# Both groups of a turn finished as (x - m)(1 + k s) + m, in a kernel of group normalization, gates and a 3x3 convolution

## The reference, cut to what matters

```python
x_n = (x - mean_group(x)) / sqrt(var_group(x) + eps)
gap, gmp = mean(gx, (h, w)), max(gx, (h, w))
channel_weight = sigmoid(gn(conv1x1(concat([gap, gmp])), over channels' pixels))
pos_h, pos_w   = gates from the row means and the column means of gx
sx = conv3x3(gx * pos_h * pos_w) + b_s3
spatial_weight = sigmoid(gn(sx) )          # mean and variance per channel, w and b
out = x + gx * (channel_weight * spatial_weight)
```

## Time and profile before

| | us |
|---|---|
| three timed runs | 3390.4, 3395.1, 3396.04 (median 3395.1) |
| the profiled execution | 3391.47 |
| its span, first to last instruction | 3389.6 |
| busy in the span: DVE, PE, ACT, POOL | 3288.2, 3212.1, 3050.6, 2542.6 |
| one turn in the steady part, first L644 to next | 25.60 |
| mean granted TensorE clock | 0.994 |

### The profile page before, as it was taken

The page is one execution under the profiler, slowest core; times in us unless marked ns, Lnnn a source line. Parts: engine busy times, 40 slices in busy tenths (PEclk is TensorE's granted clock), DMA queues, the critical chain, the costliest instruction groups (busy, mean ns, idle before and its releaser), DMA issues.

```text
span 3389.6 us, 125024 instructions
## 1 busy us (share of the span) xinstructions
PE 3212.1 (95%) x51732; PEld 1483.5 (44%) x51732; DVE 3288.2 (97%) x1997; ACT 3050.6 (90%) x5634; POOL 2542.6 (75%) x1548
## 2 busy tenths in 40 slices
PE   2999999999999999999999999999999999999996
PEld 1444444444444444444444444444444444444442
DVE  8999999999999999999999999999999999999984
ACT  1899999999999999999999999999999999999986
POOL 2777777887787777777787777777777777778872
PEclk9999999999999999999999999999999999999998
DMA  5467676776776767677677677667767767667755
GB/s 127 113 163 165 167 170 157 169 172 157 168 172 162 167 169 167 160 169 173 155 169 175 155 168 173 162 163 171 169 159 172 171 157 168 169 160 168 173 112 101
DMA packets 1115102, 545.32 MB, mean 161 GB/s; under 512 B 65712, under 2 KB 1114544, under 8 KB 1114544
## 3 DMA queue, kind: packets, MB, share of 16 engines
q1 hardware_dynamic: 836016, 403.05, 52.3%
q10 hardware_dynamic: 278528, 134.28, 14.9%
HBM read 268.63 MB, written 268.44 MB: 158 GB/s over the span
## 4 chain that ended last, share of the span: by engine, by line
DVE 58%; issue 23%; PE 7%; POOL 5%; ACT 3%; SPq 1%; DMA 1%; ACTq 1%; DVEq 0%; POOLq 0%
DVE mx L659 13%; DVE sp_buf L607 13%; DVE sums L644 12%; DVE gated L699 8%; DVE fold L632 6%; PE conv_ps L747 6%; DVE fold L636 2%; SPq L237 1%; DMA out<-sp_buf 1%; POOL rstd L327 1%; ACT sp_buf L393 1%; POOL rstd L266 1%; DVE sp_buf L617 1%; POOL var_e L308 1%; ACTq L382 1%
## 5 line engine op out<-in xcount | busy, mean ns | idle before, releaser
L747 PE MATMUL conv_ps<-gated,W_conv 64*32 64x512 f32 x49152 | 2803.4, 590 | 2.8 <-issue 1.6
L747 PEld LDWEIGHTS conv_ps<-gated,W_conv 64*32 64x32 f32 x49152 | 1126.3, 105 | 1492.5 <-issue 1461.2
L285 POOL TENSOR_TENSOR gated<-gate_w,gate_hr 128x2048 f32<-128x2048 f32 x256 | 1053.9, 4117 | 10.1
L393 ACT ACTIVATE sp_buf<-conv_ps,weights 128x512 f32<-128x512 f32 x1024 | 692.0, 678 | 148.3 <-DMA out<-sp_buf 120.6
L607 DVE SCALAR_TENSOR_TENSOR sp_buf<-xt,negm,sp_buf 128x2048 f32<-128x2048 f32 x256 | 600.3, 2345 | 42.6 <-ACT sp_buf L455 26.8
L699 DVE SCALAR_TENSOR_TENSOR gated<-xt,negm,gated 128x2048 f32<-128x2048 f32 x256 | 594.8, 2364 | 13.9 <-POOL gated L285 13.9
L327 POOL TENSOR_TENSOR rstd<-var_e,consts 128x4 f32<-128x4 f32 x129 | 389.0, 3015 | 273.4 <-DVE var_e L686 273.2
L644 DVE TENSOR_REDUCE sums<-xt 128x32 f32<-128x4096 f32 x128 | 564.9, 4413 | 0.1
L659 DVE TENSOR_REDUCE mx<-xt 128x2 f32<-128x4096 f32 x128 | 564.4, 4409 | 0.2 <-issue 0.2
L447 ACT ACTIVATE sp_buf<-sp_buf,bias,scale 128x2048 f32<-128x2048 f32 x256 | 536.9, 2097 | 8.5
L465 ACT ACTIVATE junk<-xt,negm 128x2048 bf16<-128x2048 f32 x256 | 512.5, 2002 | 28.3 <-DVE negm L693 28.3
(11 more groups left out here) (84 smaller groups left out, 2256.0 us busy)
## 6 DMA issues: line engine op xcount, KB each, us to landing
out<-sp_buf SPq DMA_DIRECT2D x2048, 128.0 KB, 2.8
xt<-in_x SPq DMA_DIRECT2D x1024, 128.0 KB, 3.7
xt<-in_x ACTq DMA_DIRECT2D x1024, 128.0 KB, 3.6
weights<-in_by_channel SPq DMA_DIRECT2D x1, 116.5 KB, 2.1
S_chan<-in_same_channel SPq DMA_DIRECT2D x1, 64.0 KB, 1.9
masks<-in_row_masks SPq DMA_DIRECT2D x1, 12.0 KB, 2.1
```

What stands on the lines that cost most here:

```text
L285: nc.gpsimd.tensor_tensor(gated[:, d, j, 1:1 + NB, 1:1 + W], gate_w[:, d, j].unsqueeze(1).to_broadcast([P, NB, W]), gate_hr[:, d, j].unsqu ...
L393: nc.scalar.activation(sp_buf[:, g, k * BB:(k + 1) * BB], conv_ps[:, k], ACT.Identity, bias=V["b_s3"], accum_out=sums2).then_inc(evac, 1)
L747: return nc.tensor.matmul(ps, lhsT, rhs, start=start, stop=stop)
```

## The change

`add_x` is gone, and both groups end with `gate_x` and `add_mean`; ACT runs `gate_plus_one` for group 0 too. ACT evicts tiles 0 and 1 with one instruction over two PSUM banks, in the place where tile 1 stood, and tiles 4 and 5 likewise; the sum of a pair goes to the column of its first tile, and the other column stays zero (hence the memset of `early_in`). On DVE, `fold_columns(e)` moves in front of `variance1(c)` and `mean1(e)`, and the finish of both groups behind them.

```diff
+            nc.gpsimd.memset(early_in[:], 0.0).then_inc(w_pool, 1)
+            pool.wait_ge(w_pool, 8)
...
+            def evacuate_pair(u, s, n):
+                j, k = n // BANKS, n % BANKS
+                g = 2 * (s % 2) + j
+                act.wait_ge(conv_mm, 8 * u + n + 2)
+                if k == 0:
+                    if later(u, 2):
+                        act.wait_ge(stored[g], 8 * RB * (u - s % 2))
+                sums2 = late_in[:, s % 2, k:k + 1] if j == 0 else early_in[:, s % 2, 1 + k:2 + k]
+                nc.scalar.activation(sp_buf[:, g, k * BB:(k + 2) * BB], conv_ps[:, k:k + 2], ACT.Identity,
+                                     bias=V["b_s3"], accum_out=sums2).then_inc(evac, 2)
...
                 load(v, vs, come, (0, 4))
-                if real(t):
-                    evacuate(t, q, 0)
                 if real(c):
                     square1(c, sc, 1, loads(k, q, 2))
                 load(v, vs, come, (1, 5))
                 if real(t):
-                    evacuate(t, q, 1)
+                    evacuate_pair(t, q, 0)
...
                 if real(b):
                     spatial_gate(b, sb_, 0)
+                    gate_plus_one(b, sb_, 0)
                 load(v, vs, come, (3, 7))
                 if real(t):
                     evacuate(t, q, 3)
-                    evacuate(t, q, 4)
-                if real(t):
-                    evacuate(t, q, 5)
+                    evacuate_pair(t, q, 4)
...
-                dve.wait_ge(sig2, n + 1)
-                if j == 1:
-                    dve.wait_ge(one_plus, u + 1)
+                dve.wait_ge(one_plus, n + 1)
...
-                if real(b):
-                    gate_x(b, sb_, 0)
-                    add_x(b, sb_, 0)
+                if real(e):
+                    fold_columns(e, se)
                 if real(c):
                     variance1(c, sc)
                 if real(e):
                     mean1(e, se)
-                    fold_columns(e, se)
-                if real(b):
-                    gate_x(b, sb_, 1)
-                    add_mean(b, sb_, 1)
+                for j in range(2):
+                    if real(b):
+                        gate_x(b, sb_, j)
+                        add_mean(b, sb_, j)
```

More of the change, by code:

```diff
@@ L255, in _ @@
             nc.gpsimd.memset(late_in[:], 0.0).then_inc(w_pool, 1)
-            pool.wait_ge(w_pool, 7)
+            nc.gpsimd.memset(early_in[:], 0.0).then_inc(w_pool, 1)
+            pool.wait_ge(w_pool, 8)
             pool.wait_ge(w_in, 16 * W_LOADS)
@@ L365, in _ @@
             act.wait_ge(w_in, 16 * W_LOADS)
-            act.wait_ge(w_pool, 7)
+            act.wait_ge(w_pool, 8)
             def first_group(v):
@@ L733, in _ @@
             pe.wait_ge(w_dve, 70)
-            pe.wait_ge(w_pool, 7)
+            pe.wait_ge(w_pool, 8)
             nc.tensor.matmul(norm_ps[:, 0:P], M_all[:, :], W_ch_m[:, :], start=True, stop=True)
```

## The result

The changed kernel takes 3567.53 us (median of 6 runs, 3565.47 to 3571.33); the kernel before, beside it, 3393.45 (3390.4 to 3396.04). The ratio is 1.0514, 95% interval 1.0503 to 1.0526: slower, inside the range of 3490 to 3610, by 17.5 us more than the 3550 predicted.

What follows compares the result with a forecast made beforehand. DVE's 25.60 us turn was taken as the bound; a loop through ACT, DVE and POOL would make it 26.81. 1.21 us in 128 turns adds 155 to 3391.5, giving 3546, or 3550 as median; range 3490 to 3610.

Steps and rivals of the forecast that it cites:

- The bound before: Kernel before: DVE's program sets the turn at 25.60 us, with PE needing 24.96 and ACT 23.86.
- DVE's saving: On DVE, add_x (2.27 us) becomes a second add_mean (1.20): 1.07 less, so 24.53 a turn.
- ACT's 2.13 us: gate_plus_one for group 0 adds 2.13 us on ACT, between the wait for group 0's power and the next T.
- the loop: ACT, DVE, POOL, ACT: 12.74 us from T to ACT's use of the power, plus 14.07, makes turns of 26.81.
- T: The moment on ACT when one gate_plus_one ends (group 1's); ACT's turn is measured from one to the next.
- the signs named in advance: Turns about 26.8, DVE idle some 2 us, ACT waiting for POOL's power nearly every turn, a pair about 1.1.
- The pair: On ACT, one eviction of 1024 columns costs 1.11 us, saving 0.21; limits were 0.32 saved and 0.68 lost.
- The store: Group 0 finishes 2.54 us later, but landings up to 10.1 after it only use up the wait for POOL.
- It follows and does not lead: PE has 1.85 us a turn to spare, so later evictions of tiles 0 and 3 do not set the turn.
- the clock: Rival, sharing 0.06 with a slow pair: the granted clock falls; a PE waiting 1.85 us had no row.
- The forecast's 1.21 us a turn: Loss per turn from the loop through POOL, in each of 128 turns: 155 us in all.
- The emptying: The last turns have no reductions, but ACT's added work lies bare, so the same 1.21 us each was kept.

Runs made afterwards that it cites:

- P: The kernel before with only the two pair evictions (tiles 0 and 1, 4 and 5) and the memset: 3397.78 us, ratio 1.0010.
- H: The kernel before with only DVE's column halvings moved ahead of variance1, mean1 and the finish of both groups: 3518.74 us, ratio 1.0369.
- F: The kernel before with only the new finish of group 0 (gate_plus_one and add_mean for both groups): 3604.01 us, ratio 1.0616.
- P and H: The changed kernel with the old finish of group 0 (add_x, no gate_plus_one), pairs and moved halvings kept: 3573.56 us, ratio 1.0527.

## Why the prediction was right, point by point

**The bound before.** DVE's program was it: P alone changes nothing, and a DVE program longer by a reduction of some 1.1 us makes the turn 1.04 longer (25.60 to 26.64).

**DVE's saving** of 1.07 us came as stated (910.5 us busy in 1000, with a mean turn of 26.99, make 24.6 a turn, predicted 24.53) and was worth nothing.

**ACT's 2.13 us and the loop.** L452 at T + 12.67 for 12.74, the rest of the turn 14.03 for 14.07: 1.11 us a turn for 1.21. That the loop runs through DVE's finish of group 1 and POOL's program is shown by two edits that touch neither ACT nor PE: the power earlier, and `add_mean` shorter. The finish alone makes the turn of 26.97. Of the signs named in advance, ACT's wait for POOL came in 77 of 97 turns and not in nearly every one, since a wait for the store ahead of the pair takes its place in others; DVE's idle time (2.35 us a turn) and the pair are as said.

**The pair** was sized right (1.11). That its place behind `square1(c, 1)` also covers the store was in the prediction only as a sum of offsets (8.86 after the finish, where tile 0 alone would wait from 7 on); with single evictions at their old places the kernel is 48 us slower.

**The store.** "It costs nothing in most turns" held: 46 waits in 97 turns, 0.43 us each turn, most within the wait for POOL; but one, of 2.21, began the ninth long turn. But it costs nothing only beside a loop that is longer. With POOL's loop opened it sets 26.35, and H alone costs 3.7%. I had costed each edit within the whole change and had not asked what H does by itself; my view after the result, that undoing F would restore the time, fell with the run of P and H.

**PE.** "It follows and does not lead" is the step that failed. It holds at the full clock. All 37 stretches at the lower level come behind a wait of PE, and adding such waits to the old kernel by DVE brought the low clock too (33 windows for 2); so the waiting brings it down. A PE at the lower level for 6.8 us uses up its 1.85 us of spare, and what it is late by goes into the loop, where POOL's held power adds to it. With the one turn that the store began this makes nine turns and 26.9 us. The prediction had the clock only among the rivals, without a row or a price.

**The number.** That the time came within 17.5 us is in part luck, as two errors have opposite signs. The forecast's 1.21 us a turn would be 147.6 in the 122 turns; the loop brought 135.4, so it was 12 too high there. The long turns and the smaller late ones, 26.9 and 3.3, were not forecast. The emptying was: 7.9, for six turns of 1.21.

**Open.** The changed kernel and the one with DVE's old order, both with a turn of 26.7, have nearly as many low stretches (37 and 43), but 8 of 6.8 us against 39; why they last longer in one isn't settled. Nor is it shown why POOL gets in between some DVE instructions and not between others (the last section).

## What to carry to other kernels

When the fullest engine is relieved by giving work to another, sum the loops and not the engines: here every engine's own work stayed below 25.60 a turn and the turn became 26.71, since the moved 2.13 us lay in a chain ACT, DVE, POOL, ACT with only 0.7 us to spare. Each moved step should be costed alone as well as in the whole, because two loops of nearly equal length hide each other: undoing the finish alone or the order alone gave nothing back (3573.6 and 3588.9 for 3567.5). A wait named at a small instruction (a power over one column) is worth following back; exchanging it with its neighbour gave back 79 us, 2.2%.

## What the runs showed of the hardware

POOL's power over 128x1 took 0.54 us during reductions (0.53 to 0.56 in all 123 of the kernel before that start in L659), and 2.71, 2.55 and 3.32 in the rows above: where it fell on `gate_x`, a DVE instruction of two tensors, with `add_mean` behind it, it ended only when both had. In the kernel before, where `add_x` followed `gate_x`, the same power took 2.40 and ended 0.4 us after `gate_x`, during `add_x`, in the turn of the earlier trace rows (POOL's timeline):

```profile
1610.12 2.40 POOL L266 TENSOR_TENSOR rstd<-var_e,consts 128x1 f32<-128x1 f32 x1 [2.48 <-ACT var_e L430]
```

So it did in 88 of the 90 cases of that kernel that start under `gate_x`. Replacing `add_x` by `add_mean` thus also lengthened what POOL can be held for. In these traces a held power got in where the next DVE instruction was one of two tensors, and then ended some 0.4 us into it: ahead of `add_x`; ahead of the first halving, when it had started under `add_mean` (40 of 41 with DVE's old order); ahead of `gate_x`, when it had started under the second halving (28 of 28 in the changed kernel). It did not get in between `gate_x` and `add_mean`, nor with two small instructions between them. The Trainium skill (GPSIMD Engine Reference, the specifications) says that the SBUF interfaces are shared with VectorE, and that the contention is with instructions of two SBUF inputs or in a 2-port mode. The rows agree for two inputs (`gate_x`) and for the reductions, which left POOL alone; `add_mean`, of one tensor, held POOL too (4.62 us for a product of 3.61), and no row shows in which mode it runs.
